# Gate and up products in Strassen form, and the normalised input made from a transposed copy of x

## The reference

```python
xn = layernorm(x)                                  # x: 1 x 2048 x 512, no affine part
# attention, on xn
h = layernorm(xn) * gamma + beta                   # a second layernorm, with eps 1e-5
q, k, v = h @ Wq, h @ Wk, h @ Wv                   # 512 x 512 each
attn = softmax(causal(q @ k.T / sqrt(512)))
a = attn @ v @ o_proj + xn
# FFN, on xn; I = 2048
u = silu(xn @ w_gate) * (xn @ w_up)
u = keep the 2 of each 4 neighbours of u with the largest magnitude, 0 elsewhere
out = x + a + u @ w_down
```

## Time and profile before

| | |
|---|---|
| median of 3 runs | 873.61 us (871.95 to 873.92) |
| span of the profiled execution | 871.7 us |
| TensorE busy | 858.8 us, 3936 instructions |
| VectorE busy | 426.9 us, 794 instructions |
| ScalarE busy | 261.6 us, 434 instructions |
| GpSimd busy | 99.0 us, 87 instructions |
| moved by DMA | 55.08 MB, mean 63 GB/s |

### The profile page before, as it was taken

One profiled execution on the slowest core, in us unless ns is written; L12 is line 12 of the kernel. 1 busy time (PEld: TensorE's weight loads), 2 busy tenths in 40 slices (PEclk: granted clock), 3 DMA queues, 4 the chain that ended last, 5 costly groups with the idle time before them and its releaser, 6 DMA issues.

```text
span 871.7 us, 10011 instructions
## 1 busy us (share of the span) xinstructions
PE 858.8 (99%) x3936; PEld 711.4 (82%) x3936; DVE 426.9 (49%) x794; ACT 261.6 (30%) x434; POOL 99.0 (11%) x87
## 2 busy tenths in 40 slices
PE   7999999999999999989999999999999999999998
PEld 5888888888888888868888888888888888888886
DVE  6566555433323322435627625627625627625626
ACT  5652433322212232132252222252222252222211
POOL 3010101000000030040051020051020041020000
PEclk9999999999999999999999999999999999999999
DMA  6316132012030058510002010002010001001102
GB/s 241 124 46 205 37 121 97 25 62 84 1 121 25 28 204 329 187 50 1 0 1 97 1 48 1 1 1 96 1 48 0 0 0 48 0 1 49 48 1 97
DMA packets 27399, 55.08 MB, mean 63 GB/s; under 512 B 2272, under 2 KB 2272, under 8 KB 26848
## 3 DMA queue, kind: packets, MB, share of 16 engines
q1 hardware_dynamic: 25776, 51.39, 16.4%
q10 hardware_dynamic: 1584, 3.15, 1.2%
HBM read 37.75 MB, written 16.78 MB: 63 GB/s over the span
## 4 chain that ended last, share of the span: by engine, by line
PE 96%; DVE 3%; ACT 0%; DMA 0%; issue 0%; SPq 0%; DVEq 0%; ACTq 0%
PE bank L498 13%; PE bank L499 13%; PE bank L500 13%; PE bank L396 12%; PE bank L398 12%; PE bank L397 12%; PE bank L516 6%; PE bank L518 6%; PE bank L517 6%; PE bank L406 3%; DVE hid L811 1%; DMA raw<-L_attn_qkv 0%; DVE beats_a L788 0%; DVE beats_b L789 0%; DVE hid L784 0%; DVE xT_lo L816 0%
## 5 line engine op out<-in xcount | busy, mean ns | idle before, releaser
L784 DVE TENSOR_TENSOR hid<-rows,bank 128x512 f32<-128x512 f32 x64 | 44.0, 687 | 236.6 <-PE bank L500 226.5
L498 PE MATMUL bank<-xT_hi,zg_hi 128*128 128x512 f32 x256 | 100.3, 392 | 2.9 <-DVE hid L784 2.9
L499 PE MATMUL bank<-xT_lo,zg_hi 128*128 128x512 f32 x256 | 100.3, 392 | 0.0
L500 PE MATMUL bank<-xT_hi,zg_lo 128*128 128x512 f32 x256 | 100.1, 391 | 0.0
L499 PE MATMUL bank<-xT_lo,mu_hi 128*128 128x512 f32 x256 | 99.8, 390 | 0.0
L498 PE MATMUL bank<-xT_hi,mu_hi 128*128 128x512 f32 x256 | 99.8, 390 | 0.0
L500 PE MATMUL bank<-xT_hi,mu_lo 128*128 128x512 f32 x256 | 99.8, 390 | 0.0
L626 ACT ACTIVATE rows<-bank 128x512 f32<-128x512 f32 x64 | 38.3, 598 | 192.3 <-PE bank L500 189.3
L518 PE MATMUL bank<-dw_hi,hs_lo 128*128 128x512 f32 x240 | 93.6, 390 | 0.0
L516 PE MATMUL bank<-dw_hi,hs_hi 128*128 128x512 f32 x240 | 93.6, 390 | 0.0
L517 PE MATMUL bank<-dw_lo,hs_hi 128*128 128x512 f32 x240 | 93.3, 389 | 0.0
(11 more groups left out here) (130 smaller groups left out, 1500.2 us busy)
## 6 DMA issues: line engine op xcount, KB each, us to landing
xnT_hi<-stage_hi SPq DMA_DIRECT2D x16, 256.0 KB, 2.2
xnT_lo<-stage_lo SPq DMA_DIRECT2D x16, 256.0 KB, 2.5
rows<-L_attn_x SPq DMA_DIRECT2D x16, 256.0 KB, 2.6
resid<-rows SPq DMA_DIRECT2D x16, 256.0 KB, 2.0
xT_hi<-xnT_hi SPq DMA_DIRECT2D x4, 1024.0 KB, 12.2
xT_lo<-xnT_lo SPq DMA_DIRECT2D x4, 1024.0 KB, 13.5
raw<-L_ffn_w_down SPq DMA_DIRECT2D x4, 1024.0 KB, 4.8
acc<-resid SPq DMA_DIRECT2D x4, 1024.0 KB, 10.3
```

The source lines that it names most:

```text
L498: pe.matmul(banks[r % 2][:], lhs_hi, rhs_hi, start=(k == 0), stop=False)
L499: pe.matmul(banks[r % 2][:], lhs_hi, rhs_lo, start=False, stop=False)
L500: last = pe.matmul(banks[r % 2][:], lhs_lo, rhs_hi, start=False, stop=(k == KT - 1))
L784: nc.vector.tensor_tensor(hid[:, r, :], rows[:, r % 2, :], up_bank[r % 2][:], ALU.mult).then_inc(hid_ready, 1)
```

## The change

**Gate and up.** The product of a weight block with two chunks of tokens is seen as a product of 2 x 2 blocks, and made with seven block products in place of eight (one level of Strassen in Winograd's form). The blocks are: 256 input features against 256, unit positions r of one parity against the other, and the two chunks of a token pair. There are two token pairs (passes), eight groups q of 256 hidden units, so N_Q = 16 steps n. In each, `gate_up(n)` makes seven fills of six matmuls for gate and seven for up, 84 matmuls. Fills accumulate on each other, and what has to be kept of a bank between two fills is copied out by ScalarE (`snapshot`); VectorE adds the sums of two banks (`add_sum`). The seven operands of the weights (A11, A12, A22 and the sums S1 to S4) are made on the chip during attention: 32 weight units and 8 units of w_down are loaded, summed by VectorE, split by ScalarE and GpSimd, and both halves stored to DRAM (`unit` steps, four stages of SBUF). The FFN loads them ready made, a set of 3.67 MB for each n. The seven operands of the tokens (B11, B21, B22, T1 to T4) are made from the stored normalised input at the start of each pass.

**Down.** `down(d)` runs two steps behind gate and up: TensorE issues gate_up(n), then down(n - 2). Its lo halves are subtracted by GpSimd for every step. Its banks are two in place of four. mag and hs_hi have the same memory. The loop over j is written out in full.

**Normalised input.** A transposed copy of x (x_t) is a further input. The row statistics are stored to DRAM and loaded spread over all partitions (`spread`); VectorE scales the transposed chunk with them, six instructions of 1024 elements. The transposes `xn_turn` and `xh_turn` are gone. The normalised chunk is stored to DRAM before its memory takes the high half of the affine result. The inputs w_gate and w_up are given in another order of elements, one array `w_units`.

The core of the diff:

```diff
@@ the order of attention
-    steps += [vo[0], vo[1], *xh_t[0][0:3], vo[2], xh_t[0][3], xn[0][0], vo[3], *xn[0][1:3], z[0][0], xn[0][3], *z[0][1:3]]
-    steps += [stats_of[1], z[0][3], v[0][0], ("scores", 0, 0), exp[0], scale_of[1], *v[0][1:3], *xh_t[1][0:2]]
+    steps += [vo[0], vo[1], xn[0], *xh[0], vo[2], vo[3], x_stats[1], z[0][0], x_scale[1], *z[0][1:3], xn[1], z[0][3], v[0][0]]
+    steps += [("scores", 0, 0), exp[0], x_stats[2], *v[0][1:3], *xh[1][0:2], x_scale[2], *some(0, 2)]
+    beside = {0: [v[0][3], exp[1], *xh[1][2:4], *some(2, 4)],
+              1: [xn[2], exp[2], v[1][0], *xh[2][0:2], *some(4, 6)],
+              2: [exp[3], *xh[2][2:4], *some(6, 9)],
+              3: [v[1][2], exp[4], *some(9, 13)],
+              4: [v[1][3], exp[5], x_stats[3], *some(13, 17)],
+              5: [exp[6], *some(17, 21)],
+              6: [exp[7], *some(21, 25)],
+              7: [exp[8], *some(25, 30)],
+              8: [*v[2][0:2], *some(30, 35)],
+              9: [v[2][2], *some(35, NU), x_scale[3]],
+              10: [v[2][3], xn[3], *xh[3]]}
@@ memory
+        mag = at("mag", 168 * KB, [P, G, W], F32)
+        hs_hi = at("hs_hi", 168 * KB, [P, G, W], F32R)
@@ SP queue
+                elif kind == "x_scale":
+                    sp.wait_ge(rstd2_ready, n + 1)
+                    sp.wait_ge(scale_ready, n + 1)
+                    sp.dma_start(row_stats_dram[n].rearrange("v t p -> p v t"), row_stat[:, n, :, :], ...)
+                    sp.wait_ge(row_stat_stored, 16 * (n + 1))
...
+                    sp.dma_start(spread[n][:], row_stats_dram[n].rearrange("v t p -> v (t p)").partition_broadcast(P))
+                elif kind == "unit":
...
+                    if n + 2 < NU:
+                        load_unit(n + 2)      # waits until unit n - 2 is stored
+                    if n:
+                        store_unit(n - 1)     # waits for its lo half, then two stores
@@ GpSimd
+            for d in range(ND):
+                for r in range(G):
+                    pool.wait_ge(hs_hi_ready, G * d + r + 1)
+                    nc.gpsimd.tensor_tensor(hs_lo[r][:], unit_of(d, r)[:], hs_hi[:, r, :].bitcast(F32), ALU.subtract)
@@ TensorE
+                block_product(0, n, A11, B11, X[0], True)
...
+                X_wait(2)
+                for m in range(2):
+                    pe.wait_ge(kept[m], 3 * n + 1)
+                    block_product(m, n, S2, T2, X[m], False)
...
+            for n in range(N_Q + 2):
+                if n < N_Q:
+                    gate_up(n)
+                if n == 1:
+                    pe.wait_ge(rows_ready, NT)
+                if n >= 2:
+                    down(n - 2)
@@ ScalarE
+            for n in range(N_Q + 2):
+                d = n - 2
+                if d >= 0:
+                    act.wait_ge(down_full, TC * d)
+                    for r in range(G):
...
+                        nc.scalar.activation(mag[:, r, :], unit_of(d, r)[:], ACT.Abs)
@@ VectorE
+                elif kind == "xn":
+                    dve.wait_ge(xt_loaded[n], 16)
+                    dve.wait_ge(spread_loaded, 16 * (n + 1))
...
+                elif kind == "unit" and not is_down(n):
+                    dve.wait_ge(unit_loaded[s], 16 * (n // STAGES + 1))
+                    nc.vector.tensor_tensor(t[:, S1, :], t[:, S3, :], t[:, A22, :], ALU.add)
```

More of the change, by code:

```diff
@@ L71, in attention_ffn @@
-    steps += [stats_of[1], z[0][3], v[0][0], ("scores", 0, 0), exp[0], scale_of[1], *v[0][1:3], *xh_t[1][0:2]]
[L73 to L76, removed]
-               11: [*z[3], *v[3]]}
[L80 to L89, removed]
+    xh, z, v = ([fills(kind, c) for c in range(NCH)] for kind in ("xh", "z", "v"))
@@ L503, in down, with block_product @@
-            def down(j, c, peeled_first=False, units=(hs_hi, hs_lo), banks=down_bank):
-                if c == 0:
-                    pe.wait_ge(wt_lo["down"], j * G + G)
+            def block_product(m, n, w_op, x_op, dst, first):
+                for kt in range(2):
+                    u = wset[n % 2][:, 2 * m + kt, :, w_op, :]
+                    x_hi, x_lo = X_hi[x_op][:, kt, :], X_lo[x_op][:, kt, :]
+                    pe.matmul(dst[:], u[:, 0, :], x_hi, start=(first and kt == 0), stop=False, skip_group_check=True)
+                    pe.matmul(dst[:], u[:, 0, :], x_lo, start=False, stop=False, skip_group_check=True)
+                    last = pe.matmul(dst[:], u[:, 1, :], x_hi, start=False, stop=(kt == 1), skip_group_check=True)
+                last.then_inc(full[m], 1)
@@ L651, in block_of_weights @@
-            def block_of_weights(j, last):
-                for c in range(1, NCH):
-                    chunk(j, c, split_next=(c == NCH - 1 and not last), split_down=(c == 1),
-                          units=last_units[0] if last and c == NCH - 1 else hs_hi)
-                if not last:
-                    chunk(j + 1, 0, False, False)
-            act.wait_ge(resid_stored, 16 * NT)
-            chunk(0, 0, False, False)
-            block_of_weights(0, False)
-            with act.Fori(1, NJ - 1) as j:
-                block_of_weights(j, False)
@@ new lines, in add_sum, with hidden @@
+            def add_sum(m, n, src, fill, dst, snaps):
+                dve.wait_ge(full[m], FILLS * n + fill)
+                dve.wait_ge(kept[m], 3 * n + snaps)
+                nc.vector.tensor_tensor(dst[:], src[:], dst[:], ALU.add).then_inc(summed[m], 1)
+            def hidden(n, result, sums, silu, up):
+                dve.wait_ge(silu_ready, 4 * n + result)
+                if sums:
+                    dve.wait_ge(summed[1], 3 * n + sums)
+                nc.vector.tensor_tensor(up[:], silu[:], up[:], ALU.mult).then_inc(hid_ready, 1)
@@ L835, in block_of_weights @@
-            def block_of_weights(j, last):
-                for c in range(1, NCH):
-                    chunk(j, c, (j, c - 1), units=last_units if last and c == NCH - 1 else (hs_hi, hs_lo))
-                if not last:
-                    chunk(j + 1, 0, (j, NCH - 1))
-                else:
-                    add_down(j, NCH - 1, last_bank)
-            chunk(0, 0, None)
-            dve.wait_ge(acc_loaded, 16 * NCH)
-            block_of_weights(0, False)
-            with dve.Fori(1, NJ - 1) as j:
-                block_of_weights(j, False)
```

924 lines of the change are left out of this document (539 added, 385 removed).

## The result

The changed kernel takes 1033.89 us (median of 4 runs, 1030.39 to 1036.08), the kernel before 873.69: a ratio of 1.183, 95% interval 1.181 to 1.186. I had said slower, 959 us, at most 1000; the direction was right, the size not. The profiled execution has a span of 1028.3 us.

A forecast was written before the change was run, and what follows sets the result against it. TensorE's instruction count was taken as the time, with no slack. From a span of 871.7 us, +94 for attention and -8.4 for the FFN gave 957.3, a median of 959 us; 8-in-10 range 903 to 1000.

The forecast's parts named there:

- The FFN's sum: All FFN changes together, from fewer matmuls to tail, start and steady losses: -8.4 us.
- the turn between the passes: FFN, change from one token pair to the next: VectorE late once, 1.5 us lost.
- the last two down steps: FFN tail: no gate and up to hide the magnitudes, which share memory with the rounded units; +31 us in all.
- The statistics' store: Normalised input: storing a chunk's row statistics to DRAM takes 4 us, between 2.0 and 7.1.
- The unit's pace: Operand units in attention: 3.9 us per weight unit, 4.9 per down unit, set by the SP queue's waits for stores.
- (a): Rival, quick transfers: statistics take 2 us, units the engines' 2.9 and 3.9; 925 us, chance 0.20.
- (b): Rival, faster: TensorE's lead covers normalisation and units whole; 852 us, chance 0.07.
- (c): Rival, shared port: GpSimd and VectorE hold each other off, 22 us in FFN, some 15 in attention; 995, chance 0.11.

The follow-up runs named there:

- e4: Changed kernel with the magnitudes of the last two down steps in other memory, ScalarE waiting for the down step before only ahead of rounding: 1034.62 us.
- e5: e4 plus VectorE making comparisons, sums and keeps of the last two down steps between the additions of the down step before: 1029.15 us.
- e9: e5 plus the down operands of the last two steps loaded earlier, into the memory of operand set 0: 1023.58 us.
- e1: Changed kernel with each chunk's statistics stored as 128 pieces of 48 B, not 1536 words of 4 B (order left wrong): 1002.76 us.
- e3: Changed kernel with all 40 operand units made before the first weight split, none beside attention: 1160.12 us.
- e6: e3 with the unit loads issued one step later, as in e2: 1102.17 us.
- e2: Changed kernel with the SP queue loading unit n+1 instead of n+2 in step n, so awaiting stores issued two steps earlier: 1018.23 us.
- e11: Seven-product FFN with e9's tail and the old kernel's normalisation; weight units spread to other places in attention, down units made in the FFN: 902.52 us.

## Why the prediction was right or wrong

- **What bounds the kernel, and the sign**: right. TensorE had no slack: z[3] is 164 us late against the kernel before, the last rows 172.
- **The FFN's sum**: -8.4 forecast, -9.5 measured. That it is so near is in part luck: the steps take 30.3 us (30.0 and 3 us in all for 14 of them were forecast), the turn between the passes costs 3.5 (1.5), and the last two down steps take 26.1 and 25.2 (26.4 each, with the lower clock). The stated reason for these was incomplete. I named the shared memory of magnitudes and rounded units; e4, e5 and e9 show that and, behind it, the order on VectorE and the single buffer of the down operands. Mending only what I had named gains 3 us.
- **The statistics' store**: the term that failed first. I took 4 us between 2.0 and 7.1, by the bytes; it is 8.5 to 12.5, outside even the upper bound, and e1 shows that it goes with the number of pieces. Four times 4.5 to 8.5 too little make 26 us. The Trainium skill, DMA: Bandwidth & Descriptors, section Specifications, says that below 512 B a transfer becomes a read-modify-write; that rule alone does not tell the two stores of e1 apart, since words of 4 B and pieces of 48 B both lie below it, and the latter cost 1.5 to 2.2 us where the former cost 4 to 7 times as much. I had the rule in the text and gave it no weight, since it names no time.
- **The unit's pace**: 3.9 taken within 2.9 to 4.3, measured 5.1; 4.9 within 3.9 to 5.5 for a down unit, measured 7. From unit 13 on that is 18 x 1.2 + 8 x 2.1 = 38 us. This is the larger of the two terms that failed. The prediction had the wait itself (both stores of the unit before must land) and mis-sized it. Its upper bound, 2.9 for the bytes and 1.35 for a store's fixed part, is the landing of the second store, which the profile puts at 4.3 us; but that store is issued 0.85 us after the load of its step (219.18 and 220.03 above), the next load follows only its landing (224.24), and issue and landing add up to 5.1 in each step. In a down unit the second store lands after 6.0 to 6.3 us, which with the same 0.85 is near 7. e3 shows the pace without any neighbour, e6 takes it away. In attention e2 gives back 16 of the 38, and the queue waits for GpSimd's low halves instead. The Trainium skill, DMA: Bandwidth & Descriptors, section Anatomy of one DMA, from which the prediction takes 2.0 us plus bytes, is on transfers that GpSimd issues. These are issued by SyncE, so neither the 4.1 us a unit nor the disagreement seen in the prediction tests that line.
- 26 and 38 are 64 of the 71 us by which the span was missed (1028.3 against 957.3). The rest arises early: the queue is 26 us late at unit 13, of which three stores explain 17, and the unit loads from 120.1 to 192.0 us stand 6.5 us apart on average. What makes these slow is not settled. The median stands 5.6 us above the span, not 1.9, because the profiled execution was the fastest of the four.
- **The rivals**: (a) and (b) fell with the same two numbers. (c), the shared port, was priced at 22 us for the FFN, which came out 1.1 us under my forecast, and at some 15 in attention. Its mechanism is there: in e11 each second step is 1.9 us longer, and in the changed kernel's attention 12 of VectorE's 128 unit sums last 1.0 to 2.2 us in place of 0.29, 19 us in all. Whether these 19 reached TensorE no run tells. The units' pace of 5.1 is not from it: in e3 only 3 of the sums are held, and the pace is the same.
- **The range** reached to (a) and (c), somewhat beyond the bounds of the two transfer prices (935 to 985; by them the lower end is 925, 8 and 26 us off 959), and both prices lay outside their bounds. The error was to call the nearest row a bound where its shape (rows of 2 KB, 12 times fewer pieces; no second store beside it) was another.

## What to carry to other kernels

A transfer of many small pieces was priced here by its pieces, and a loop on a queue by what each step waits for that was issued in the step before; neither is seen in bytes over rate. Work that other engines did beside TensorE was free up to a count per tile (four units here), so it has to be spread, and placed where the engines that serve TensorE have nothing urgent queued behind it. When a wait has one named cause, look for what would end next behind it: the tail here had three.

## What the runs showed of the hardware

- A store of 1536 words of 4 B from 128 partitions landed in 8.5 to 11.8 us (behind the unit stores in up to 13.6) in the seven traces that have it, the same 6 KB as 128 pieces of 48 B in 1.5 to 2.2 (5.5), as 12 rows of 512 B in 1.3 to 1.7 (5.5).
- In these rows a VectorE instruction with two operands in SBUF that begins during one of GpSimd ends only after it: 0.69 us became 2.90 beside a subtraction of 2.72, and in the changed kernel 0.29 became 2.2 beside one of 2.13:

```profile
261.92 2.22 DVE L835 TENSOR_TENSOR u_raw<-u_raw 128x128 f32<-128x128 f32 x1
264.06 2.20 DVE L836 TENSOR_TENSOR u_raw<-u_raw 128x128 f32<-128x128 f32 x1
```

  GpSimd has two subtractions there, from 261.87 for 4.25 us. A comparison that had begun 0.23 us before GpSimd kept its 0.69 (L1027 at 545.46 in e11_hybrid_spread), and so did an addition that reads a PSUM bank (0.68, L951 at 555.88); what decides was not tried.
- Loads and stores together moved 324 GB/s for 102 us in e6_first_later, where the units run alone.
- After the two waits of 12.01 us TensorE's matmuls start 0.42 to 0.61 us apart for 6.0 and 3.8 us (granted clock 0.50 from 985.8 to 991.0), then 0.23 again: its two levels.
